# A graph network's node run: one leaky maximum made by VectorE in columns, its way back to rows by plain transposes

## The reference, cut to what matters

```python
h = relu(layernorm(x))
y = layernorm(h) * ln_gamma + ln_beta
out = y @ cheb_w[0] - y @ cheb_w[2]            # the propagated terms are zero
h = leaky(out + cheb_b, 0.01)                  # where(v >= 0, v, 0.01 * v)
xh = (h @ gat_w).reshape(n, 4, 64)             # 4 heads
# a node whose only edge is its own loop: every head's weight is 1
o = leaky(mean(xh, axis=1) + gat_b, 0.01)
x1 = x + o                                     # then the second layer's part: x2 = x1 + layernorm(...)
```

## Time and profile before

| | before |
|---|---|
| time, median of 3 runs (lowest to highest) | 8187.95 us (8158.64 to 8191.77) |
| the profiled execution's own time | 8203.84 us |
| its span, first to last instruction | 8201.9 us |
| mean granted TensorE clock | 0.696 |
| span of the node run | about 1040 to 2840 us |

### The profile page before, as it was taken

One profiled execution on the slowest core, in us unless ns is written; L12 is line 12 of the kernel. 1 busy time (PEld: TensorE's weight loads), 2 busy tenths in 40 slices (PEclk: granted clock), 3 DMA queues, 4 the chain that ended last, 5 costly groups with the idle time before them and its releaser, 6 DMA issues. The chain is left out here.

```text
span 8201.9 us, 78150 instructions
## 1 busy us (share of the span) xinstructions
PE 4544.7 (55%) x17175; PEld 2185.1 (27%) x17176; DVE 4298.6 (52%) x6828; ACT 2273.9 (28%) x4663; POOL 4255.4 (52%) x3989
## 2 busy tenths in 40 slices
PE   2139946566565656657775553775885443555100
PEld 0014434344343433322221111332332111122000
DVE  1027745555554555534430008996996444787433
ACT  0000034444444422211112221232332112565211
POOL 6650044444444365556646652555664665665566
PEclk6569977777777767765556666887887555777555
DMA  0000022222222223321112222332232333222221
GB/s 12 0 0 17 0 72 86 86 90 88 85 86 85 90 66 73 78 51 50 50 50 70 76 75 67 101 103 58 77 82 72 104 102 91 58 64 55 60 63 51
DMA packets 444561, 541.92 MB, mean 66 GB/s; under 512 B 207490, under 2 KB 221960, under 8 KB 443641
## 3 DMA queue, kind: packets, MB, share of 16 engines
q1 hardware_dynamic: 319050, 449.36, 18.1%
q0 software_dynamic: 125440, 91.77, 5.7%
HBM read 302.04 MB, written 276.42 MB: 71 GB/s over the span
## 5 line engine op out<-in xcount | busy, mean ns | idle before, releaser
L1028 POOL DMA_INDIRECT l_got<-d_x,l_near x1176 | 1236.0, 1051 | 780.5 <-issue 384.2
L1028 POOL DMA_INDIRECT ln_xd<-in_x,ln_near x392 | 391.2, 998 | 1344.8 <-issue 865.5
L720 PE MATMUL ps<-hot_lo,hot_w 128*128 128x512 bf16 x2351 | 568.2, 406 | 441.2 <-issue 342.8
L1028 POOL DMA_INDIRECT p_got<-d_ext,p_near x392 | 399.5, 1019 | 348.1 <-DMA p_near<-in_src_rows 213.3
L662 DVE SCALAR_TENSOR_TENSOR hot_w<-iota_hi,hiS,vals 128x384 bf16<-128x384 bf16 x392 | 242.4, 618 | 589.2 <-remote 364.6
L1028 POOL DMA_INDIRECT p_got<-d_tx,p_near x392 | 399.4, 1019 | 275.1 <-issue 232.8
L1028 POOL DMA_INDIRECT p_got<-d_h,p_near x392 | 396.1, 1010 | 257.1 <-DMA p_near<-d_ls 134.2
L2218 POOL DMA_INDIRECT out<-fi_res,fi_near x392 | 381.6, 973 | 259.1 <-issue 171.7
L1187 DVE TENSOR_TENSOR_SCAN p_sums<-same,p_sums,ps 65x1024 f32<-65x1024 f32 (+3 forms) x98 | 229.4, 2341 | 498.7 <-remote 245.8
L606 POOL DMA_INDIRECT d_pos<-place,near x392 | 386.0, 985 | 167.8 <-issue 162.1
L1658 POOL TENSOR_TENSOR at_own<-at_hd,at_al 128x2048 f32<-128x2048 f32 x49 | 269.9, 5509 | 383.0 <-ACT at_al L1752 358.7
(11 more groups left out here) (371 smaller groups left out, 11827.7 us busy)
## 6 DMA issues: line engine op xcount, KB each, us to landing
d_x<-ln_x SPq DMA_DIRECT2D x196, 256.0 KB, 2.2
l_xd<-d_x SPq DMA_DIRECT2D x147, 256.0 KB
d_ext<-ln_ext SPq DMA_DIRECT2D x98, 264.0 KB
ln_x<-in_x SPq DMA_DIRECT2D x98, 256.0 KB
d_h<-ln_hb SPq DMA_DIRECT2D x98, 256.0 KB, 2.1
d_x<-l_x SPq DMA_DIRECT2D x98, 256.0 KB
out<-d_x SPq DMA_DIRECT2D x49, 512.0 KB
l_got<-d_x,l_near POOLq DMA_INDIRECT x1176
```

The source lines that it names most:

```text
L720: last = nc.tensor.matmul(bank(h), hot_w[:, r, k], hot_lo[:, r, 512 * h:512 * h + 512], start=False, stop=False)
L1028: nc.gpsimd.indirect_dma_start(out=out[:, q], out_offset=None, in_=source, in_offset=bass.IndirectOffsetOnAxis(ap=ids[:, q:q + 1], axis=0) ...
```

## The change

ScalarE makes only the slanted part, 0.01 v + 0.01 b, into a new buffer `slant`. VectorE makes the maximum itself, max(v + b, slant), from bank 2 and `slant` into the one buffer `hf`: a new stage `h` in the third list (group s - 2) at number 3, which is behind norm b's three sums (number 2). The product with `gmean` is then one product in place of two, and the way back to rows is four plain transposes in place of eight products. So ten fp32 products become one and four transposes. `uf`, the second leaky maximum, stays as it was.

```diff
-        hf, uf = ([t(f"{n}{k}", [P, HALF])[:] for k in (0, 1)] for n in ("hf", "uf"))
+        slant, hf = t("slant", [P, HALF]), t("hf", [P, HALF])
+        uf = [t(f"uf{k}", [P, HALF])[:] for k in (0, 1)]
...
+                def h(i, r, g):
+                    yield 3
+                    dve.wait_ge(m["slanted"], g + 1)
+                    after(dve, m["h_rows"], g)
+                    nc.vector.scalar_tensor_tensor(out=hf[:], in0=bank(2), scalar=W.base_b[:], in1=slant[:], op0=ALU.add,
+                                                   op1=ALU.max).then_inc(m["h_done"], 1)
...
-                ring_loop(dve, NODE_GROUPS, [a, indices], [], [], [b, take], [scale_b], [c])
+                ring_loop(dve, NODE_GROUPS, [a, indices], [], [h], [b, take], [scale_b], [c])
...
                     hold(pe, m["h_done"], g + 1)
-                    for k in (0, 1):
-                        last = nc.tensor.matmul(bank(3), W.gmean[:], hf[k], start=k == 0, stop=k == 1)
-                    last.then_inc(m["mean_done"], 1)
+                    nc.tensor.matmul(bank(3), W.gmean[:], hf[:], start=True, stop=True).then_inc(m["mean_done"], 1)
                     yield 3
                     hold(pe, m["hb_done"], g)
-                    sum_transposed(nc, bank(6), hf, W, S // 2).then_inc(m["h_rows"], 1)
+                    for q in range(S // 2):
+                        at = slice(P * q, P * q + P)
+                        last = nc.tensor.transpose(bank(6)[:, at], hf[:, at], W.ident[:])
+                    last.then_inc(m["h_rows"], 1)
...
                     act.wait_ge(m["base_done"], g + 1)
-                    after(act, m["h_rows"], g)
-                    leaky_parts(nc, hf, bank(2), 0.01, W.base_slanted[:, 0:1], W.base_slanted[:, 1:2]
-                                ).then_inc(m["h_done"], 1)
+                    after(act, m["h_done"], g)
+                    nc.scalar.activation(slant[:], bank(2), ACT.Identity, scale=0.01, bias=W.base_slanted[:, 0:1]
+                                         ).then_inc(m["slanted"], 1)
```

More of the change, by code:

```diff
@@ L823, in lone_nodes @@
         yaf, ybf = (t(n, [P, HALF]) for n in ("yaf", "ybf"))
-        hf, uf = ([t(f"{n}{k}", [P, HALF])[:] for k in (0, 1)] for n in ("hf", "uf"))
+        slant, hf = t("slant", [P, HALF]), t("hf", [P, HALF])
+        uf = [t(f"uf{k}", [P, HALF])[:] for k in (0, 1)]
         near, xd, dd = t("near", [P, 2, S], I32), t("xd", [P, 2, S, C]), t("dd", [P, 2, S])
         norm_a, norm_b = (NormTwice(sem, t, n, bank(7)[:, 32 * k:32 * k + 32]) for k, n in enumerate("ab"))
-        names = ("ya_done", "ya_t", "yaf_done", "base_done", "h_done", "mean_done", "u_done", "u_rows", "x1_done",
+        names = ("ya_done", "ya_t", "yaf_done", "base_done", "slanted", "h_done", "mean_done", "u_done", "u_rows", "x1_done",
                  "yb_done", "yb_t", "ybf_done", "residual", "x2_done", "h_rows", "hb_done", "tabbed", "near_done",
```

## The result

On the chip of the prediction the changed kernel takes 8082.47 us (median of 4 runs, 8071.52 to 8105.69). The kernel before takes 8189.86 us there (4 runs). The ratio is 0.9875, with an interval of 0.9846 to 0.9904: **1.25% faster, where I had forecast 1.3% slower**, and outside the range. Two rivals, both faster, had stood at 8122 and 8119.

The account below looks back on a forecast made before the run. No engine was full; pairs of steps, 36.7 us each, were taken as pinned to GpSimd's gather run by TensorE's late reports. 47 x 2.2 = 103, about 5 for the ends: 8188 + 108 = 8296 us, range 8115 to 8365.

Parts of the forecast that it names:

- Two rivals: Node run: rows of `h` stay the first late report, 8122 us, chance 0.18; or short steps rule, 8119 us, chance 0.06.
- late reports: While gathers run, TensorE work ending after about +4.6 us from a pair's first gather is told late: first +17, rest +23.1.
- The step that failed: Long step of a pair: the residual becomes first late report, about +17; rows of `h` come with the rest at +23.1.
- The cover that I had counted as gone: Work from `hb` to the next step's beginning, done free between +17 and +23 before, now falls after +23.1.
- The rule under that step: While gathers run, what TensorE finishes later than about +4.6 us after a pair's first gather is told to others late.
- The first rival: Long step: residual passes, rows of `h` stay first late report, `hb` at +17.3; 1.4 us less per pair, 8122 us, chance 0.18.
- The main sum: Node run: `hb` at +23.1, `gmean` at +28.7, pair 38.9 against 36.7 us; 47 x 2.2 = 103, +108 us with ends.
- first after +4.6: Reading that a report is the first late one for ending first after +4.6 us, not for which product it is.
- forecast 2.2 us at half clock and 1.16 us: Way back to rows by four transposes, 1.3 to 2.2 us less; one ScalarE activation out of the chain before `hb`, 1.16 us.

Follow-up runs that it names:

- maximum_first_b: Changed kernel with VectorE's maximum at the head of its step: 8066.72 us, ratio 0.9825, on a late chip; first run, prompt chip, 6241.77 us, 0.9985.
- products_first: Changed kernel with the maximum at the head of its step and four fp32 identity products instead of the four transposes: 8137.84 us, ratio 0.9901, late chip.

## Why the prediction was wrong

**Right:** the reading that the pair is pinned to the gather run by late reports of TensorE. `gmean` 5.6 us behind `hb`. The residual ending at +6.9, and so becoming the first late report. One VectorE instruction of 0.74 us where I had taken 0.69. The wait moved from `hf` to `hb`. `ybf` at +22.8 where I had +23.1.

**The step that failed** is the one that says "The rows of `h` are now second, and come with the rest at +23.1". I had seen one early and several late reports, and made "first" and "rest" of them. In the trace after, two come early: the residual's lets `x2` start at +9.9, only 3.0 us after its products end, not at +17; and that of the rows of `h` lets `hb` start at +12.8 (middle values), before even the +17 of the old kernel. So `hb`, the root of norm a, `ya`, its transposes and `gmean` are all done by +21.1. The cover that I had counted as gone was there, and `gmean`'s later place lies in it at no cost. `maximum_first_b` shows that cost to be nothing: 34.8 us in both.

The rule under that step, that what ends later than +4.6 is told late, doesn't hold either. In five of 42 pairs of the changed kernel the residual ended as late as +9.2 to +9.6 and was reported at once. In the one whose first gather is at 1284.83:

```profile
1292.36 2.07 PE L807 MATMUL ps<-cm,ln_ybf 128*128 128x128 f32 x8
...
1294.47 0.69 DVE L945 TENSOR_TENSOR ln_x<-ln_x,ps 128x512 f32<-128x512 f32 x1 [1.98 <-PE ps L807]
```

Everything built on that step falls: the chain doesn't start with `hb` at +23.1 (15.8 us to the next gather), but with `ybf` at +22.8 (12.0 us). Its pair of 38.9 us was 34.8, and the +2.2 us a pair were -1.8.

**The first rival had the mechanism, and its number by luck.** It had `hb` early (at +17.3, measured +12.8), the base product held by `yaf` until about +25 (measured +24.9), and a chain of base, betas, residual, transposes, `hb`. Its pair was 33.3 us because it let the clock rise at +28.2. The clock in the pair shown, 1834 to 1836 and 1840 to 1842 us (last but two of the columns):

```profile
1834.00:1836.00 2.00, 1.83 (x2) 0.50 (x2) 0.54 (x1) 2.00 (x5) 0.00 (x0) 0.50 0.64 221
1840.00:1842.00 2.00, 2.00 (x14) 2.00 (x12) 0.84 (x2) 0.89 (x3) 0.00 (x0) 0.60 0.02 7
```

It is at 1.2 GHz until +31 to +33; TensorE had stood idle for 3.8 us before +24.9. That makes 34.8. So in a pair like the one that the prediction read, 34.7 us before, the change gains nothing; the rival took 1.4 us off just this pair, and came within 40 us of the measured time because other pairs, which it didn't look at, got shorter. The main sum had the opposite slip: it built the new pair from that one of 34.7, and set it against the mean of 36.7. I gave the rival 0.18 and took "first after +4.6" for the better account of the same rows. Its condition ("as soon as the residual's report is on time") wasn't quite met either; both reports are late, only by less.

**Where the gain comes from.** Rows of before that the prediction passed over show it best. In each sixth pair, where GpSimd pauses behind the first gather, `hf` came already at +8.7 in the old kernel. So nothing of it was late there that is early now, and this pair (first gather 1285.74) compares like with like:

```profile
1310.27 0.60 ACT L1021 ACTIVATE ln_ybf<-ps 128x512 f32<-128x512 f32 x1 [12.32 <-DMA d_pos<-place,near]
...
1312.37 2.04 PE L950 MATMUL ps<-ln_yaf,w02c 128*128 128x512 f32 x2 [10.71 <-ACT ln_yaf L998]
...
1318.21 3.42 PE L351 MATMUL ps<-ident,ln_hf 128*128 128x128 f32 x16
...
1321.72 0.69 ACT L341 ACTIVATE ln_hf<-ps,base_slanted 128x512 f32<-128x512 f32 x1 [6.84 <-PE ps L351]
...
1322.88 0.60 ACT L1012 ACTIVATE ln_hb<-ps 128x512 f32<-128x512 f32 x1
```

From `ybf` to the next gather (1325.81) are 15.5 us, and 12.0 in the changed kernel: 3.42 - 1.06 = 2.4 us by the transposes and 1.2 us by `hf` no longer standing ahead of `hb`. The pair is 40.1 us before and 36.2 after. In the other pairs the old kernel was helped by its own lateness. `hb` at +18.4 put `gmean` right in front of the base product, TensorE wasn't idle, and the clock was up for the rows of `h`: 34.3 us in the shortest, even 0.5 less than after. Where `hf` came as late as +20.8, `gmean` held up the base product and the pair was 37.3. The gain is the sum over these: 26 us from the seven sixth pairs (3.4 to 4.0 us each), 13 us from the second and third pair of the run, 47 us from the other 38, which range from 0.5 us longer to 4.1 us shorter. So the terms of the change were sized about right (forecast 2.2 us at half clock and 1.16 us, measured 2.4 and 1.2); what was wrong was which chain they stand in.

**Why the reports of the rows of `h` come earlier now isn't settled.** Their products ended at +6.3 before, +7.4 after. `hf` started at +17.2 (middle value), `hb` after the change at +12.8, in `products_first` at +11.4, in `maximum_first_b` at +9.9. Two comparisons take one difference alone. `products_first` and `maximum_first_b` differ in the products against the transposes: the rows of `h` end at +6.3 and +6.2, and `hb` starts 1.5 us apart. The changed kernel and `maximum_first_b` differ in the place of the maximum: the rows end 1.2 us apart, and `hb` starts 2.9 us apart. So both TensorE's amount of work and its place have a part; by what mechanism isn't shown. Nor do I know what in a late chip differs from a prompt one.

The Trainium skill ("Perfetto Trace Analysis", Tensor Engine Instruction) was cited for the shown end of a matmul not being its report. The trace after agrees on a late chip, 7.4 against 13.5 us in the pair shown. On a prompt chip the two can't be told apart: the semaphore is raised within 0.01 us of the shown end.

## What to carry to other kernels

When an interval is pinned by something that you can't explain, price the change in each chain that could be the one behind the pin, and look first at pairs in which the trace itself varied the suspected cause: here each sixth pair already held the answer, 15.5 us of chain at half clock. Set a forecast for one interval against that same interval, not against the mean. Here work ahead of the pin was free and work behind it counted in full, so ask of each moved instruction on which side it lands, and not how long it is. And a gain of 1% that rests on an unexplained wait may belong to the chip: the same diff is 1.25% faster where reports are late and 0.5% slower where they aren't, and of the versions tried on both kinds `maximum_first` is the one that is faster than the kernel before on either (0.9825 and 0.9985).

## What the runs showed of the hardware

- The same kernel takes 6253 to 6255 us on some chips and 8188 to 8215 us on others. In the node run the difference is bound to GpSimd's indirect gathers: without them the changed kernel's node run takes 984 us on either (first to last transpose of `yb`); with them the kernel before takes 1019 us on the one and 1756 on the other (first to last row gather). For the other stages this wasn't tried.
- On the slower chips TensorE's semaphores are raised up to 16.3 us after its instruction ended (149 of 528 updates of the kernel before are over 0.5 us late), while GpSimd issues gathers with 0.3 us between them. ScalarE's and VectorE's are not late, by 0.01 us at most. A pause of 1.8 us lets TensorE's through, 7745 us instead of 8067; on the other chips the same pause costs 82 us (6324 against 6242), and no report is late there.
- GpSimd issues one gather of 128 rows in 1.3 us (1.00 busy, 0.30 idle), so 16 bound a pair at 20.8 us although the engine shows busy for only 76% of the time (kernel before, prompt chip).
- Four fp32 products by the identity take 1.06 us at full clock and 1.91 at half; four transposes 0.60 and 1.06.
